# First attention of a fused two-layer block: the inverted softmax sums go through DRAM scratch and not through TensorE transposes

## The reference, cut to what matters

```python
# x: (8, 128, 512), ctx: (8, 128, 512), all fp32
x = x + L0_xattn(layernorm(x), ctx)     # 32 query heads of 16, 8 key/value heads, then @ Wo
x = x + L0_ffn(layernorm(x))            # 512x512 + bias + a LoRA of rank 16 chosen by batch element
x = x + L1_xattn(layernorm(x), ctx)     # 16 heads of 32, softmax over batch*head (axis 0)
x = x + L1_ffn(layernorm(x))            # 512x512 + two encoders through an inverse FFT

# L0_xattn, the part the change touches
scores = einsum('bhqd,bhkd->bhqk', q, k) * scale
probs  = softmax(scores, axis=-1)       # the division by the row's sum is what moves
out    = einsum('bhqk,bhkd->bhqd', probs, v).transpose(0, 2, 1, 3).reshape(b, sq, 512) @ Wo
```

## Time and profile before

| what | value |
|---|---|
| runs, device time | 293.88 us median of 3 (293.35 to 294.14) |
| span of the profiled execution, first to last instruction | 292.5 us |
| lies around the span (median of the runs less the span) | 1.4 us |
| PE busy | 284.9 us, 97% |
| DVE / ACT / POOL busy | 234.3 / 167.4 / 146.6 us |
| DMA | 39.5 MB, mean 135 GB/s |
| granted TensorE clock | 1.00 |

### The profile page before, as it was taken

One profiled execution on the slowest core, in us unless ns is written; L12 is line 12 of the kernel. 1 busy time (PEld: TensorE's weight loads), 2 busy tenths in 40 slices (PEclk: granted clock), 3 DMA queues, 4 the chain that ended last, 5 costly groups with the idle time before them and its releaser, 6 DMA issues.

```text
span 292.5 us, 6282 instructions
## 1 busy us (share of the span) xinstructions
PE 284.9 (97%) x2136; PEld 224.2 (77%) x2136; DVE 234.3 (80%) x358; ACT 167.4 (57%) x284; POOL 146.6 (50%) x194
## 2 busy tenths in 40 slices
...
GB/s 224 348 224 277 147 210 146 242 182 256 90 252 233 170 128 94 148 255 20 103 100 51 135 26 131 57 60 145 172 107 156 109 72 38 2 0 3 108 89 92
DMA packets 35784, 39.52 MB, mean 135 GB/s; under 512 B 3928, under 2 KB 21848, under 8 KB 35754
## 3 DMA queue, kind: packets, MB, share of 16 engines
...
...
## 4 chain that ended last, share of the span: by engine, by line
PE 81%; DVE 7%; POOL 4%; issue 3%; ACT 2%; DMA 1%; POOLq 0%; DVEq 0%; ACTq 0%
PE ps L494 16%; PE ps L496 15%; PE ps L495 15%; PE ps L783 5%; PE ps L693 5%; PE ps L859 4%; PE ps L750 3%; PE ps L772 3%; PE ps L898 3%; PE ps L871 2%; PE ps L796 1%; PE ps L909 1%; DMA out<-XB 1%; PE ps L706 1%; DVE xn L1225 1%
## 5 line engine op out<-in xcount | busy, mean ns | idle before, releaser
L1464 POOL TENSOR_TENSOR slot_l<-stg,slot_h 128x512 fp32r<-128x512 f32 x19 | 25.3, 1343 | 41.9 <-ACT slot_h L967 41.9
L1260 DVE TENSOR_REDUCE mx<-ps 128x8 f32<-128x1024 f32 x32 | 38.1, 1214 | 2.5 <-PE ps L750 2.2
L494 PE MATMUL ps<-xT_h,slot_h 128*128 128x256 f32 x128 | 36.9, 288 | 0.0
L496 PE MATMUL ps<-xT_h,slot_l 128*128 128x256 f32 x128 | 36.0, 281 | 0.0
L495 PE MATMUL ps<-xT_l,slot_h 128*128 128x256 f32 x128 | 35.9, 281 | 0.0
L1046 ACT ACTIVATE PT<-ps 128x1024 f32<-128x1024 f32 x32 | 31.2, 1026 | 4.2 <-PE ps L772 4.1
L1476 POOL TENSOR_SCALAR var_eps<-moments 128x1 f32<-128x1 f32 x32 | 7.5, 235 | 41.8 <-DVE moments L1221 40.9
L1506 POOL TENSOR_TENSOR zpart<-P 128x512 f32<-128x512 f32 x16 | 21.2, 1323 | 10.8 <-ACT P L1123 9.8
L1123 ACT ACTIVATE P<-ps 128x1024 f32<-128x1024 f32 x16 | 16.4, 1025 | 17.0 <-PE ps L871 17.0
L494 PEld LDWEIGHTS ps<-xT_h,slot_h 128*128 128x128 f32 x128 | 24.2, 189 | 1.7 <-issue 0.4
L992 ACT ACTIVATE xT_h<-ps 128x512 fp32r<-128x512 f32 x24 | 14.1, 600 | 18.3 <-PE ps L693 15.4
...
## 6 DMA issues: line engine op xcount, KB each, us to landing
ctx_in<-in_ctx SPq DMA_DIRECT2D x20, 256.0 KB, 3.0
QS<-Q_h SPq DMA_DIRECT2D x16, 256.0 KB, 3.3
o_dram<-OTs SPq DMA_DIRECT2D x16, 256.0 KB, 2.2
...
X<-in_x SPq DMA_DIRECT2D x8, 256.0 KB, 5.4
stg<-in_wq SPq DMA_DIRECT2D x8, 256.0 KB, 5.1
QS<-Q_l SPq DMA_DIRECT2D x8, 256.0 KB, 3.2
O<-o_dram SPq DMA_DIRECT2D x8, 256.0 KB
```

Source lines behind the costliest of these rows:

```text
L494: eng.matmul(dst, left[0], right[0], start=start, stop=False)
L496: return eng.matmul(dst, left[1], right[0], start=False, stop=stop)
L1260: dve.tensor_reduce(mx[:, b % 2, :].rearrange("p (x r) -> p r x", r=REP)[:, r, :], wide(step).rearrange("p k (g t) -> p (k g) t", g=4), AX ...
L1464: pool.tensor_tensor(lo, src, hi.bitcast(F32), ALU.subtract).then_inc(w_lo_pool, 1)
```

## The change

Each step keeps its name, but what stands behind the Z steps is new. `ZR` copies the sum rows of OTs to z_in as 128 partitions of 32 values. DVE `ZT` inverts z_in into z_inv. Two new SP steps follow: `ZW` stores z_inv in DRAM (z_dram, 16 KB) once the inversion is done, and `ZL` reads it back twice, each time into 64 partitions of z_wide (128 KB each) in which every row of 2 KB is repeated 16 times; it waits for the store's landing and for the multiplication of b - 1. DVE `ZB` multiplies O by z_wide. The PE steps `ZT` and `ZB`, the ACT step `ZE` and the tile zin are gone. `OX` and `SM` wait on a new counter, `o_scaled`, in place of the freed bank.

```diff
+            z_in, z_inv = s1("z_in", [D // HD0]), s1("z_inv", [D // HD0])
+            z_wide = s1("z_wide", [D])
+        z_dram = nc.dram_tensor("z_dram", (B, 4, 2, D), F32, kind="Internal").ap()
 ...
                     consumed(sp, ("PV", b, 0))
                     consumed(sp, ("PV", b, 1))
-                    sp.wait_ge(zin_set, 1)
                     if b:
-                        filled(sp, ("ZT", b - 1))
-                    sp.dma_start(zin[0:KVH * REP, :], OTs[HD0:P:2 * HD0, :, :]).then_inc(z_loaded, 16)
+                        sp.wait_ge(z_inverted, b)
+                    sp.dma_start(z_in[:, :], OTs[HD0:P:2 * HD0, :, :]).then_inc(z_loaded, 16)
+                elif kind == "ZW":
+                    b = step[1]
+                    sp.wait_ge(z_inverted, b + 1)
+                    sp.dma_start(z_dram[b], z_inv[:, :]).then_inc(z_stored, 16)
+                elif kind == "ZL":
+                    b = step[1]
+                    sp.wait_ge(z_stored, 16 * (b + 1))
+                    if b:
+                        sp.wait_ge(o_scaled, b)
+                    for gq in range(2):
+                        sp.dma_start(z_wide[gq * HALF:(gq + 1) * HALF, :],
+                                     z_dram[b][:, gq, :].unsqueeze(1).broadcast_to([4, HD0, D])).then_inc(wide_loaded, 16)
 ...
-                elif kind == "ZT":
-                    pe.wait_ge(z_loaded, 16 * (b + 1))
-                    pe.transpose(dst[:, 0:P], zin[:, :], ident[:, :]).then_inc(psum_full, 1)
-                elif kind == "ZB":
-                    pe.wait_ge(wide_ready, b + 1)
-                    for r in range(REP):
-                        last = pe.transpose(dst[:, r * P:(r + 1) * P], z_wide[:, r, :, :].rearrange("p g d -> p (g d)"),
-                                            ident[:, :])
 ...
-                elif kind == "ZE":
-                    act.activation(z_wide[:, :, :, :], rec[:, :, :].unsqueeze(3).broadcast_to([P, REP, KVH, HD0]),
-                                   ACT.Copy).then_inc(wide_ready, 1)
 ...
                 elif kind == "ZT":
                     b = step[1]
-                    filled(dve, step)
+                    dve.wait_ge(z_loaded, 16 * (b + 1))
                     if b:
-                        dve.wait_ge(wide_ready, b)
+                        dve.wait_ge(z_stored, 16 * b)
-                    dve.reciprocal(rec[:, :, :].rearrange("p r (x j) -> p r x j", x=2),
-                                   place(step)[:, 0:KVH * REP].rearrange("p (j x r) -> p r x j", x=2, r=REP)).then_inc(dve_freed, 1)
+                    dve.reciprocal(z_inv[:, :], z_in[:, :]).then_inc(z_inverted, 1)
                 elif kind == "ZB":
-                    filled(dve, step)
                     dve.wait_ge(u_loaded, 16 * (b + 1))
-                    dve.tensor_tensor(O[:, :], O[:, :], place(step), ALU.mult).then_inc(dve_freed, 1)
+                    dve.wait_ge(wide_loaded, 32 * (b + 1))
+                    dve.tensor_tensor(O[:, :], O[:, :], z_wide[:, :], ALU.mult).then_inc(o_scaled, 1)
```

All five lists are written anew, and with them many banks. Of the lists the diff's rows that matter are these (POOL's start, SP's start, and two stretches of SP):

```diff
-POOL: SET.1 SET.2 SET.0 LNs.0.0 LNs.0.1 L.wkv.1 L.wq0.0
+POOL: SET.0 SET.2 SET.1 LNs.0.0 LNs.0.1 L.wq0.0 L.wkv.1
-SP:   LX.0 LX.1 LC.0.0 LW.wkv.0 LI LW.wkv.1 LC.0.1 LW.wq0.0
+SP:   LX.0 LI LX.1 LW.wq0.1 LW.wkv.1 LC.0.0 LW.wq0.0 LW.wkv.0
-SP:   OW.0.1 ZR.0 OW.0.0 QL.2 OR.0 DM.2
+SP:   OW.0.0 OW.0.1 QL.2 ZR.0 ZW.0 LC.0.7 OR.0 ZL.0 DM.2
-SP:   OW.6.0 OW.6.1 ZR.6 OR.6 OW.7.0 OW.7.1 ZR.7 LC.1.2 OR.7 LC.1.3
+SP:   ZR.6 OW.6.1 OW.6.0 ZW.6 ZL.6 OR.6 OW.7.1 OW.7.0 ZR.7 ZW.7 OR.7 LW.wq1.2 LW.wq1.0 ZL.7
```

More of the change, by code:

```diff
@@ L90 @@
-W.wbase.2 W.wbase.0 V1.4 CT.2.3 FP.3 CT.2.0 FP.1 V1.5 V1.2 CT.2.1 PV1.6 V1.3 PV1.7 PV1.4 V1.0 PV1.5 FP.0 LNn.3.6
-V1.1 XT.3.6 PV1.3 PV1.2 LNn.3.7 XT.3.7 LNn.3.4 XT.3.4 PV1.0 PV1.1 XT.3.5 XT.3.2 LNn.3.3 XT.3.3 XT.3.0 XT.3.1
+SET.8 LNn.0.0 W.wq0.1 XT.0.0 XT.0.1 W.wq0.0 W.wkv.0 W.wkv.1 V0.0 V0.1 W.wq0.2 K0.0 W.wq0.3 CT.0.2 Q0.0.0 Q0.0.1 CT.0.3
+LNn.0.3 V0.2 W.wo.3 LNn.0.2 XT.0.3 V0.3 XT.0.2 K0.1 MT.0 CT.0.4 W.wo.1 LNn.0.4 W.wo.0 Q0.1.0 CT.0.5 Q0.1.1 ST.0.1
+ST.0.0 ST.0.3 ST.0.2 XT.0.4 MT.1 XT.0.5 PV.0.0 PV.0.1 W.wo.2 Q0.2.0 ST.1.3 ST.1.1 ST.1.2 MT.2 ST.1.0 PV.1.1 Q0.2.1
@@ L92 @@
+CT.2.1 PV1.6 V1.0 FP.0 PV1.4 PV1.5 LNn.3.6 V1.1 XT.3.6 PV1.2 PV1.3 LNn.3.7 XT.3.7 LNn.3.4 PV1.0 PV1.1 XT.3.4 XT.3.5
+XT.3.2 LNn.3.3 XT.3.3 XT.3.0 XT.3.1
 """
 DVE_TEXT = """
[L95 to L97 removed]
@@ L120 @@
-NM.4 L.wbase.2 L.wbase.0 LNs.3.6 XB.6 LNs.3.7 NM.1 NM.3 LNs.3.4 XB.7 LNs.3.2 LNs.3.5 LNs.3.3 XB.4 XB.5 LNs.3.1
-LNs.3.0 XB.2 XB.3 XB.0 XB.1
+SET.0 SET.2 SET.1 LNs.0.0 LNs.0.1 L.wq0.0 L.wkv.1 L.wq0.2 L.wq0.3 KM.0 LNs.0.2 LNs.0.3 CL.0.3 LNs.0.4 KM.1 KM.2 L.wo.1
+LNs.0.5 KM.3 LNs.0.6 L.wo.2 L.wo.0 LNs.0.7 CL.0.6 KM.4 CL.0.7 KM.5 LNs.1.1 KM.6 KM.7 LNs.1.0 L.w0.0 L.w0.2 LNs.1.2
+L.w0.1 CL.1.0 LNs.2.0 L.wk1.1 L.wk1.0 LNs.1.3 SET.5 CL.1.1 L.wk1.2 LNs.2.1 LNs.1.5 LNs.1.4 LNs.2.3 L.wq1.1 L.wq1.0
+SET.4 LNs.1.6 LNs.2.2 LNs.2.5 LNs.1.7 ZP.0 ZP.1 ZP.2 LNs.2.4 ZP.3 CL.1.4 LNs.2.7 ZP.4 ZP.5 LNs.2.6 ZP.6 ZP.7 L.wv1.2
@@ L151 @@
 DVE_FREES = {s: n for n, s in enumerate(
-    s for s in DVE_ORDER if s[0] in ("XT", "K0", "Q0", "MX", "ZT", "ZB", "WO", "F0", "OX1", "LT", "K1", "Q1", "V1", "F1", "FH", "WE"))}
+    s for s in DVE_ORDER if s[0] in ("XT", "K0", "Q0", "MX", "WO", "F0", "OX1", "LT", "K1", "Q1", "V1", "F1", "FH", "WE"))}
 HALVES = numbered(ACT_ORDER, "CT", "K0", "XT", "Q0", "OX", "LT", "K1", "Q1")
```

147 lines of the change are left out of this document (64 added, 83 removed).

## The result

| what | before | changed |
|---|---|---|
| runs, device time | 293.85 us (median of 4) | 333.75 us (median of 4, 331.65 to 335.85) |
| span of the profiled execution | 292.5 us | 334.1 us |
| mean granted TensorE clock | 1.000 | 0.959 |
| DMA | 39.5 MB | 41.75 MB |

The changed kernel is slower: ratio 1.136, 95% interval 1.130 to 1.143, so 39.9 us. The prediction had the sign (297.0 us, 3.1 more), but under a tenth of the size, and 333.75 lies far above its range of 291.4 to 300.6.

What follows compares the result with a forecast made beforehand. PE was taken as a full conveyor that bounds the kernel. 292.5 - 4.5 + 1.6 + 3.0 + 0.5 + 1.5 + 1.0 = 295.6 us of span, plus 1.4 for the median, gave 297.0 us, range 291.4 to 300.6.

Steps and rivals of the forecast that it cites:

- the price of the new path: First attention: stops of 3.0, 0.5, 1.5 and 1.0 us, from path length against the room of each b.
- cost nothing: First attention: b = 0, 2 and 3 have 14 to 16 us of room and add no stop before WO.
- What leaves the belt: On PE: removing 8 ZB steps and 8 ZT transposes saves 4.5 us, bounds 4.4 and 7.3.
- The start: Kernel start: V set last delays PE's unread matmuls, XT and V0.0; +1.6 us, bounds 1.2 and 2.2.
- ZR 2.2, ZW 2.2: Sums path from PV to WO: each of these small DMAs takes 2.2 us, 3.0 as upper bound.
- ZL, 4.9: Sums path: ZL with the first of its two issues takes 4.9 us, bounds 2.8 and 6.3.
- The stops: PE stops: 3.0 us at b = 1 and 2, 0.5 at b = 4 and 5, 1.5 at WO.6, 1.0 at WO.7.
- The rewritten order: QX and second attention: the rewritten order saves and costs something unknown; set at 0, bounds -1 and +1 us.
- The multiplication: DVE, multiplying O by the inverted sums: unchanged from before at 0.69 us, counted as 0.7 in the path.
- Rival B: First attention: SP and the DMA queues become the bound, DM.2 and QL landing behind ZL; 300.5 us, chance 0.19.
- Its sign: First attention: ST waiting on DMAs for b = 3 to 7 as well would show that Rival B holds.

Runs made afterwards that it cites:

- e14: The kernel before, in its old orders and banks, with transposes, ZR, ZW, ZL and inversion cut out and the multiplication waiting for O alone: 292.94 us (0.997).
- e4: The changed kernel in its rewritten orders, with ZR, ZW, ZL and inversion cut out and z_wide set to 1 once: 300.76 us (1.025).
- e6: The changed kernel with all DMAs and the inversion, but no computing engine waits for z_wide; each ZL waits for the one before: 320.35 us (1.090).
- e15: e7 in the orders and banks of the kernel before, ZW and ZL right behind OR: 313.5 us (1.067).
- e3: The changed kernel's way with the sums in the orders and banks of the kernel before, ZW and ZL right behind OR: 339.07 us (1.154).
- e13: e7 with ZL issued by ACT into its own queue, right behind its copies of PV.b: 321.9 us (1.099).
- e2: The changed kernel with POOL setting V first again and the early loads in their old places: 334.49 us (1.140).
- e7: e6 with SP's waits for the path taken away and all bytes kept; each ZL still waits for the previous landing: 311.84 us (1.062).
- e8: e6 with SP's waits kept, but ZL carrying 4 rows per DMA, not 64, so 16 KB in all: 304.74 us (1.038).

## Why the prediction was right or wrong

The sum of the 39.9 us as the runs give it: the transposes and the rest of the old way gone, -0.65 (e14); the rewritten orders, +7.8 (e4 less e14); DMAs and SP's waits on which no computing engine's result hangs, +19.6 (e6 less e4), where the waits alone cost 4.0 and the bytes alone 11.1; the wait for z_wide itself, +13.4 (change less e6). Together 40.2. The shares hold for this order of taking away. In the old orders they are -0.65, +20.6 for the traffic without SP's waits (e15), and +25.6 for SP's waits and the wait for z_wide together (e3 less e15).

The step that failed above all is the price of the new path: 3.0 + 0.5 + 1.5 + 1.0 = 6.0 us of stops, each from the length of one b's path against the room of that b, with ZL at 4.9 us and nothing for the transfers behind it. The runs showed 33.0 us in its place (change less e4), 19.6 of them with no computing engine waiting for z_wide. PE made eight stops of 2.0 to 5.8 us there, 27.2 in all, two of them at b = 3 (2.3 before its ST, 2.05 before WO.3), of which the prediction said that it "cost nothing". Two further steps failed: the rewritten order at 0, and the -4.5. Term by term:

- **What leaves the belt, -4.5: wrong by 3.9.** The size of the steps was nearly right: at K0.3 three ZBs and three ZTs had given 1.3 us, 0.43 for each pair, where -4.5 has 0.56. The step that failed is "so it is worth 3.5 to 5.0 us in all", which holds only if nothing else is just in time. The rows of WO.6 had told me that it was; I used this for the new path and not for the gain. e14 shows WO.2 and WO.7 at nearly their old times, set by DVE's chain and the read of O. There is chance in the size: a DVE operation beside POOL and a late store filled the room that the transposes left.
- **The start, +1.6: right in the trace, in part by luck.** PE's unread matmuls begin at 3.77 for 3.9 foretold, V0.0 at 10.17 for 10.1. But XT started only 1.2 us later than before (8.65), and V0.0 waited 0.5 us for the wkv that the prediction took to be covered; the two made up the 1.6. The first projection was still 1.7 us late (14.59 for 12.88). That it cost as much in the end no run shows.
- **ZR 2.2, ZW 2.2: right only when alone.** For b = 6, 2.0 us passed from ZR's issue to the inversion, and 2.6 from its end to ZL's issue. Behind a ZL they took more: the ZR of b = 7 was issued at 149.89 and inverted at 155.21, the ZW of b = 5 was issued at 123.50 and ZL, which waits for it, at 130.10 us.
- **ZL, 4.9: this term failed, twice.** The pair took 6.0 to 9.5 us by the landings, at or above my bound of 6.3 in seven of eight. And I priced it by itself, with O as landed, though the new list has `ZL.6 OR.6`. From ZL's issue to the multiplication of b = 6 it was 8.4 us; O landed 7.2 us after its issue there, 1.3 behind ZL, and 4.2 before.
- **The stops, 3.0 + 0.5 + 1.5 + 1.0: most places were right, their sizes and their list were too small.** Before ST of b = 2, I had up to 1.0; it was 4.15, and WO.1 then had no stop. WO.4 had 3.7 for the 0.5 foretold at b = 4 and 5, WO.6 had 3.1 for 1.5, and WO.7 had 5.8 for 1.0. The sum counted stops of WO and one of ST. It had no term for the ST of later b, nor for ACT standing before OX with the copies of PV behind it (e6: 8.6 us of PE in one wait).
- **The rewritten order, set at 0, bounds -1 and +1: wrong by some 6 without the path.** It costs 7.8 us there, the start among it, which had its own term of 1.6. The waits shown under e14 are most of it. With the path it is 5.3 us better than the old one.
- **The multiplication, 0.7 unchanged, from SBUF now:** it took 0.69 us in seven of eight and 1.64 for b = 1, and before, from PSUM, never over 0.69.
- **Rival B** had the mechanism: DMA queues as the bound, DM and QL landing behind ZL, ST waiting. Its sign, ST waiting on DMAs for b = 3 to 7, came true for b = 3 alone. Its price, 3 to 4 us more, was 1.4 us times the places where WO stops. It left out what the runs show at every b: each WO.b is 2.5 to 5.5 us later still than the one in front of it.
- **The clock** had no term at all. It is 13.7 us of PE's time in the trace. Filler in seven stops gave back 8 of them and some 3 us of the 40; the rest was not tried.

Open remain: queue against engines (e13), the start's share (e2), the share of the one wait left in e7, and why DM.0, issued at 27.8 us in both, landed at 34.1 in the changed kernel and at 31.3 in e8, with the same order up to there. The second step of ST.0 follows it (35.86 and 33.92).
